# Earlier first norm, reordered loads and unused products in the waits of the first and last image

## The chip, the core and the metric

The kernel runs on one core of a Trainium2 chip. The metric is the device time of one launch in microseconds (us). The engines of the core work side by side and meet at semaphores: TensorE (PE in the rows, its weight loads PEld), VectorE (DVE), ScalarE (ACT), GpSimd (POOL) and SyncE (SP), which here issues the transfers.

## What is computed

A small vision transformer on 64 images. Of each image: 196 patches of 768 numbers are normalised and multiplied by a 768x192 matrix, normalised again and given a class token (197 tokens of 192). Then one attention layer with 12 heads of 64, and a second one with 12 heads of 16 whose weights are corrected by a mixture of eight small experts.

```python
p = x.reshape(B, C, 14, 16, 14, 16).transpose(0, 2, 4, 3, 5, 1).reshape(B, 196, 768)
h = layernorm(layernorm(p, g1, b1) @ W + b, g2, b2)
h = concatenate([cls, h], axis=1)
h = h + attention1(layernorm(h))     # softmax((q k^T) / scale), 12 heads of 64, then w_out
h = h + attention2(layernorm(h))     # qkv + top-2 expert correction, 12 heads of 16, then Wproj
```

## The kernel before

**Stages.** Each image runs through a fixed list of steps, named in the text `ORDER` (L51): X (squares of the patches), EMB (embedding product), LA, LB, LC (two norms on DVE; POOL makes each reciprocal root at L519 and L522), T1 (transpose of the normed tokens), QK.0 to QK.2 (queries and keys), S and PS (sums of squares), N (scaling), SM.0 to SM.5 (maxima of the scores), NT, V.0 and V.1, ST (scores again, with exponentials on ACT), PV, OP, and the same for the second attention with names that end in 2. `@4` behind a step is the PSUM bank in which it starts. Steps marked `+` belong to an image half a pass ahead, `-` and `=` to images one and two half passes behind. A pass holds two images, s=0 and s=1, so 64 images take passes 0 to 31, with a "start" pass ahead that does only X, EMB, LA, LB and LC of the very first image, and a "last" pass behind that does what is left of the last two. The last half of the last pass has nothing but the second attention of image s=1, so its steps only wait for one another.

**Order within an engine.** Every engine walks the same list and runs its own part of each step in that order, waiting on semaphores. On PE each step first waits for its setup (L572 to L581: T1 of the first image for `norm_loaded`, QK.0 for `setup_dve` 3, V.0 for `setup_dve` 4, OP for 5), then for its PSUM banks to be read out (L583 to L585), and then, in its branch, for its operands.

**Loads.** SP issues `emb_loads` (embedding weights, its norm's gain and bias), the first image, `norm_loads` (token bias, the matrix `mats_sb` that holds the identity for transposes, the constants `tokc` of the second norm, `rowc`), `qk_loads` (1536 KB of `w_qk` and three small ones), `v_loads`, the second image and the rest (L447 to L455).

**DVE at the start.** It scales `emb_w` (L907), then in the start pass waits for `qk_loaded` and splits `w_qk` into a high and a low float16 part (`split_rows`, L923 and L926). Then come `constants_of_embedding` (L916, L917; it waits for `norm_loaded` and for PE), EMB (L1038 to L1045), LA (L1055, then `variance`, L1009 and L1012), LB (L1063, L1068, `variance`) and LC (L1018), and directly behind LC of the first image `weights_of_scores` (L937 to L964), which raises `setup_dve` to 3. DVE's part of T1 (L1082) stands behind that. `weights_of_attention2` (L973) stands behind T1 of s=1.

Of the kernel before, what the change touches and what calls it, by code (L numbers as in the profile page):

```python
# [26 lines left out]
B, D, NP = 64, 192, 196  # L27
NT = NP + 1
# [7 lines left out]
ITERS = B // 2  # L36
# [44 lines left out]
WIDE = ("QK", "V", "SM", "ST", "PV")  # L81
QUAD = ("SM2", "ST2")
EBUFS = 4


def banks(p):
# [67 lines left out]
def vit_tower(nc, x_t, w_emb, ln1, ln1_bias, tok_const, tok_bias, w_qk, w_v, w_out, w_gl, w_qkv2, w_lora_b,  # L154
# [4 lines left out]
    with ctx:  # L159
# [10 lines left out]
        emb_w = sb("emb_w", [128, KC, D + 1])  # L170
        ln1_sb = sb("ln1_sb", [128, KC])
        tokc = sb("tokc", [TR, 2, 2, D])
# [5 lines left out]
        qk_w = sb("qk_w", [128, 3, 2 * INNER], F16)  # L178
# [9 lines left out]
        rowc = sb("rowc", [TR, 2 * D + NE + NE * RANK])  # L188
        mats_sb = sb("mats_sb", [128, 261])
# [86 lines left out]
        emb_raw = flat(qk_sq, 128, 0, KC, D)  # L276
        ln1b_raw = flat(qk_sq, 128, KC * D, KC, TR)
# [64 lines left out]
        def wait(eng, now, sig, p, earlier=None, by=1):  # L342


            n = now.count(steps[sig[0]], p, earlier)
            if n is not None:
                eng.wait_ge(sig[1], n * by)
# [19 lines left out]
            body(Pass("last", ITERS))  # L367


        emb_loads = [(emb_raw, w_emb), (ln1_sb, ln1), (ln1b_raw, ln1_bias)]  # L370
        norm_loads = [(tok_b, tok_bias), (mats_sb, mats), (tokc, tok_const), (rowc, row_const)]
        qk_loads = [(scale_sb, scale), (sel_raw[0:64], head_rows[64:128]), (sel_raw[64:128], head_rows[64:128])]
        v_loads, loads = [], [(lorab_raw, w_lora_b), (proj_w[:, 2:3, :], w_proj[:, 2:3, :])]
        for j in range(4):
# [48 lines left out]
        @block.sync  # L423
        def _(sp):
            def load_group(group, loaded):
                for dst, src in group:
                    sp.dma_start(dst[tuple(slice(None) for _ in src.shape)], src).then_inc(loaded, 16)

            def load(n, s):
                sp.dma_start(xb[s][:], x_t[bass.ds(n * 2 + s, 1)].rearrange("b p c t -> (b p) c t")  # L430
                             ).then_inc(x_loaded[s], 16)

            def body(now):
                for kind, s, i in now.steps():
                    if kind == "QK" and i == 0 and now.which in ("first", "middle"):

                        wait(sp, now, pe_sig["EMB"], ("EMB", s, 0))
                        wait(sp, now, xsq_ready, ("X", s, 0))
                        load(now.it + 1, s)
                    elif kind == "OP2":  # L440
                        wait(sp, now, res_ready, ("OP2", s, 0))
                        dst = out[bass.ds(now.image((kind, s, i)) * 2 + s, 1)].rearrange("b t d -> (b t) d")
                        sp.dma_start(dst[1:1 + TO], res[s][0:TO, 0, :]).then_inc(stored[s], 16)
                        sp.dma_start(dst[1 + TO:NT], res[s][0:TO, 1, :]).then_inc(stored[s], 16)
                        sp.dma_start(dst[0:1], res[s][TO:TR, 1, :]).then_inc(stored[s], 16)

            load_group(emb_loads, emb_loaded)  # L447
            load(0, 0)
            load_group(norm_loads, norm_loaded)
            load_group(qk_loads, qk_loaded)  # L450
            load_group(v_loads, v_loaded)
            load(0, 1)
            load_group(loads, consts_loaded)
            sp.wait_ge(bias_cleared, 2)
            load_group(bias_loads, consts_loaded)  # L455
            passes(sp, body)
            for s in range(2):
                sp.wait_ge(stored[s], 48 * (ITERS + s))
# [69 lines left out]
        def _(pe):  # L528
# [38 lines left out]
            def body(now):  # L567
                for p in now.steps():
# [14 lines left out]
                    freed = [(b, *now.previous(users[b], p)) for b in banks(p)]  # L583
                    for sig, q, earlier in dict.fromkeys((*reader(q, b), earlier) for b, q, earlier in freed):
                        wait(pe, now, sig, q, earlier)  # L585
                    if kind == "EMB":
                        pe.wait_ge(x_loaded[s], (now.image(p) + 1) * 16)
                        for t in range(2):
# [308 lines left out]
        def _(dve):  # L897
# [13 lines left out]

            def constants_of_embedding():
                spare = next(b for b in range(8) if b not in [BANK[(k, s, 0)] for k in ("EMB", "T1") for s in range(2)])
                dve.wait_ge(norm_loaded, 16 * len(norm_loads))
                dve.wait_ge(setup_pe, 1)
                nc.vector.tensor_copy(emb_cs[:], psum[0:TR, spare, 0:D])  # L916
                nc.vector.tensor_tensor(emb_b[:], tok_b[:, 0, :], psum[0:TR, spare, D:2 * D], ALU.add  # L917
                                        ).then_inc(setup_dve, 1)
                dve.wait_ge(setup_dve, 2)
# [11 lines left out]
            def split_rows(w, raw):  # L931

                return split_weights(lambda v: w[:, v], raw[:, 0])
# [88 lines left out]
            def body(now):  # L1022
                dve.sem_clear(dve_chain)
                count[0] = 0
                if now.which == "start":
                    dve.wait_ge(qk_loaded, 16 * len(qk_loads))
                    split_rows(qk_w, qk_raw)
                for p in now.steps():
                    kind, s, i = p
                    done = rd_sig[kind][1] if kind in rd_sig else None  # L1030
                    b = BANK[p]
                    if kind == "EMB":
                        if s == 0 and now.image(p) == 0:
                            constants_of_embedding()
# [269 lines left out]
```

## Time and profile before

| what | value |
|---|---|
| median of 3 runs | 3115.53 us (3112.74 to 3116.41) |
| the profiled execution itself | 3115.51 us |
| its span from first to last instruction | 3113.7 us |
| around the span | 1.8 us |
| PE busy | 2965.3 us, 95% |
| DVE busy | 2328.8 us, 75% |
| ACT busy | 1963.5 us, 63% |
| POOL busy | 591.9 us, 19% |
| mean granted clock of TensorE | 0.987 of full speed |

All times in the rows are us from the start of the span. A granted clock of 1.00 is 2.4 GHz, and 0.50 is 1.2 GHz; a value between is a stretch in which it changed. A float32 product shows as two matmul records, a float16 product as one.

### The profile page before, as it was taken

Reading aid. Unit: us, or ns where it says so; the run is one execution under the profiler, and the core shown is the slowest. Engines: PE = TensorE matmul, PEld = TensorE weight load, DVE = VectorE, ACT = ScalarE, POOL = GpSimd, SP = SyncE. Lnnn points to the kernel's source line nnn. Section 1 sums busy time; section 2 is a strip of 40 time slices with the busy share of each in tenths; the row PEclk is TensorE's granted clock in tenths of the full one; section 3 lists DMA queues with packets and bytes.
Section 4 is the critical chain, followed back from the end, with each engine's and each line's share of the span. In section 5 each row is a group of like instructions: output and inputs, shape, how many; then the busy total and the mean of one; then the engine's idle time right before and its main releaser. Section 6 shows DMA issues by size and latency. Waiting matters only on the chain.

```text
span 3113.7 us, 98361 instructions
## 1 busy us (share of the span) xinstructions
PE 2965.3 (95%) x41624; PEld 2430.5 (78%) x41624; DVE 2328.8 (75%) x5441; ACT 1963.5 (63%) x3777; POOL 591.9 (19%) x859
## 2 busy tenths in 40 slices
PE   4899999999999999999999999999999999999996
PEld 4778877877877877877877888778778778778775
DVE  5777777777777777787777777777777777777773
ACT  2566666666666666666666666666666666666663
POOL 2111121121121121121121121121111111111210
PEclk7999999999999999999999999999999999999998
DMA  4000000000000000000000000000000000000000
GB/s 116 9 22 12 22 22 12 21 22 12 21 22 12 22 22 12 22 21 12 22 21 12 22 22 12 22 17 16 22 14 19 22 12 21 22 12 22 14 4 7
DMA packets 28389, 61.28 MB, mean 20 GB/s; under 512 B 4210, under 2 KB 18389, under 8 KB 27958
## 3 DMA queue, kind: packets, MB, share of 16 engines
q1 hardware_dynamic: 27958, 54.98, 6.1%
q8 instruction: 337, 5.52, 0.8%
q14 instruction: 94, 0.77, 0.1%
HBM read 45.29 MB, written 9.68 MB: 18 GB/s over the span
## 4 chain that ended last, share of the span: by engine, by line
PE 59%; DVE 35%; ACT 3%; issue 3%; DMA 0%; SPq 0%; POOL 0%; DVEq 0%; ACTq 0%
PE psum L686 9%; DVE mx L1118 8%; PE psum L695 8%; PE psum L590 8%; PE psum L612 7%; PE psum L622 4%; PE psum L722 4%; PE psum L674 3%; PE psum L656 3%; DVE st L1009 3%; DVE mx L1131 2%; PE psum L725 2%; DVE qk L1210 2%; PE psum L732 2%; DVE late L1227 2%
## 5 line engine op out<-in xcount | busy, mean ns | idle before, releaser
L850 ACT ACTIVATE ebufs<-psum 99x788 f32<-99x788 f32 x768 | 592.0, 823 | 58.1 <-PE psum L674 45.1
L519 POOL TENSOR_TENSOR veps<-mv,eps_ln 99x2 f32<-99x2 f32 x256 | 116.1, 453 | 2274.1 <-DVE mv L1040 1352.3
L1131 DVE TENSOR_REDUCE mx<-psum 99x4 f32<-99x788 f32 x384 | 357.5, 974 | 137.7 <-PE psum L639 137.4
L1118 DVE TENSOR_REDUCE mx<-psum 99x4 f32<-99x788 f32 x384 | 362.9, 974 | 52.1 <-PE psum L631 52.1
L612 PE MATMUL psum<-hn_s,qk_w 128*128 128x197 f16 x3840 | 354.9, 249 | 14.2 <-DVE hn_s L1082 7.2
L612 PEld LDWEIGHTS psum<-hn_s,qk_w 128*128 128x128 f16 x3840 | 323.0, 98 | 34.9 <-DVE qk L1210 19.0
L686 PE MATMUL psum<-ebufs,vx 98*32 98x197 f32 (+1 forms) x6144 | 293.6, 330 | 0.0
L695 PE MATMUL psum<-out_w,qk 128*99 128x192 f32 x1536 | 263.8, 329 | 0.1
L590 PE MATMUL psum<-emb_w,xb 128*99 128x193 f32 x1536 | 263.9, 327 | 0.0
L590 PEld LDWEIGHTS psum<-emb_w,xb 128*99 128x99 f32 x1536 | 249.1, 166 | 1.8 <-issue 1.4
L686 PEld LDWEIGHTS psum<-ebufs,vx 98*32 98x32 f32 (+1 forms) x6144 | 201.2, 110 | 57.5
L695 PEld LDWEIGHTS psum<-out_w,qk 128*99 128x99 f32 x1536 | 245.1, 166 | 0.3 <-issue 0.3
L622 PE MATMUL psum<-v_w,hn_s 128*99 128x384 f16 x1280 | 234.1, 330 | 0.0
L656 PE MATMUL psum<-qh,kh 64*99 64x197 f16 x1536 | 208.5, 255 | 17.5 <-DVE mx L1131 17.0
L1101 DVE TENSOR_TENSOR qk<-qk,ss 128x1182 f32<-128x1182 f32 x64 | 89.0, 1391 | 168.0 <-ACT ss L826 168.0
L802 ACT ACTIVATE qk_sq<-psum 128x788 f32<-128x788 f32 x192 | 158.8, 827 | 70.6 <-PE psum L612 70.6
L656 PE MATMUL psum<-ql,kh 64*99 64x197 f16 x1536 | 202.1, 246 | 0.0
L660 PE MATMUL psum<-neg_t,head_sel 64*99 64x197 f16 x1536 | 201.9, 246 | 0.0
L656 PE MATMUL psum<-qh,kl 64*99 64x197 f16 x1536 | 201.8, 245 | 0.0
L622 PEld LDWEIGHTS psum<-v_w,hn_s 128*99 128x99 f16 x1280 | 155.0, 127 | 47.1
L831 ACT CAST kh<-qk 128x1182 f16<-128x1182 f32 x64 | 75.6, 1181 | 176.4 <-DVE qk L1106 176.4
L1148 DVE TENSOR_TENSOR qk<-psum,rinv 128x394 f32<-128x394 f32 x192 | 108.9, 567 | 102.8 <-ACT rinv L861 62.1
(172 smaller groups left out, 6444.3 us busy)
## 6 DMA issues: line engine op xcount, KB each, us to landing
xb<-x_t SPq DMA_DIRECT2D x64, 591.0 KB, 3.9
out<-h SPq DMA_DIRECT2D x128, 73.5 KB
out<-h SPq DMA_DIRECT2D x64, 0.8 KB
vx<-w_qk SPq DMA_DIRECT2D x2, 384.0 KB, 11.2
qk_sq<-w_emb SPq DMA_DIRECT2D x1, 576.0 KB, 3.7
vx<-w_qk SPq DMA_DIRECT2D x1, 576.0 KB, 8.3
out_w<-w_out SPq DMA_DIRECT2D x8, 72.0 KB
late<-w_lora_b SPq DMA_DIRECT2D x1, 480.0 KB
```

Source lines behind the costliest of these rows:

```text
L590: nc.tensor.matmul(ps(p, slice(0, TR), slice(194 * t, 194 * t + D + 1)), xb[s][:, c, tile_cols(t)], emb_w[:, c, :], start=(c == 0), stop=( ...
L612: mm = nc.tensor.matmul(ps(p, slice(0, 128), slice(at, at + NT), m // 2), qk_w[:, w, f:f + 128], hn_s[s][:, v, c, 0:NT], start=(n == 0), s ...
L622: mm = nc.tensor.matmul(ps(p, slice(0, TR), slice(0, INNER // 2), b), hn_s[s][:, v, c, tile_cols(i)], v_w[:, w, INNER // 2 * b:INNER // 2 ...
L656: nc.tensor.matmul(ps(p, slice(0, TR), slice(NT * t, NT * t + NT), e), left[r], right[r], start=(n == 0), stop=False)
L660: mm = nc.tensor.matmul(ps(p, slice(0, TR), slice(NT * t, NT * t + NT), e), head_sel[r, 2 * i + e, :], neg_t[s][r, 0:NT], start=False, sto ...
L686: mm = nc.tensor.matmul(ps(p, slice(32 * j, 32 * j + 32), slice(NT * (c % 2), NT * (c % 2) + NT), c // 2), left, eb[0:n, j % 2, t, :], sta ...
L695: mm = nc.tensor.matmul(ps(p, slice(0, TR), slice(D * t, D * t + D)), o_t[s][:, m, tile_cols(t)], out_w[:, m, :], start=(m == 0), stop=(m ...
L722: nc.tensor.matmul(o, qkv2_w[:, w, f], hn2_s[s][:, v, c, 0:NT], start=(n == 0), stop=False)
L802: nc.scalar.activation(qk_sq[:, 4 * i:4 * i + 4, :].rearrange("p (b m) t -> p b (m t)", b=2), src, ACT.Square, scale=1 / WS)
L850: nc.scalar.activation(ebuf[n].rearrange("p e a t -> p e (a t)"), psum[0:TR, b + 2 * half:b + 2 * half + 2, 0:2 * NT], ACT.Exp).then_inc(r ...
L1118: nc.vector.tensor_reduce(mx[s][:, :, 2 * i:2 * i + 2].rearrange("p a e -> p e a"), psum[0:TR, b:b + 2, 0:2 * NT].rearrange("p e (a t) -> ...
L1131: nc.vector.tensor_reduce(mx2[s][:, :, at:at + 2].rearrange("p a e -> p e a"), psum[0:TR, b + 2 * half:b + 2 * half + 2, 0:2 * NT].rearran ...
```

## The change

Four things. The token bias is loaded with `emb_loads`, ahead of the first image, and `qk_loads` are issued ahead of what is left of `norm_loads`. DVE's `split_rows` of `w_qk` with its wait moves from the head of the start pass to behind LA, ahead of LB of the first image, and the wait for `norm_loaded` moves there from `constants_of_embedding`. PE runs products without use: in the first images 24 ahead of T1 (s=0), 9 and 2 ahead of QK.0 (s=0, s=1), 9 and 4 ahead of PS, 2 ahead of each of SM.0, 2, 3, 4 and 5 of both, 3 and 1 ahead of NT; in image s=1 of the last pass 3 ahead of each SM2, 8 ahead of NT2, 2 ahead of each ST2 and each PV2, and 4 ahead of OP2. Each is a float32 product of 128x128 weights with 193 columns of `emb_w`, written to the step's own first bank, which the step then overwrites. They stand behind the waits for setup and banks and ahead of the waits for operands.

```diff
+FILL_FIRST = ({"T1": 24, "QK": 9, "PS": 9, "SM": 2, "NT": 3}, {"QK": 2, "PS": 4, "SM": 2, "NT": 1})
+FILL_LAST = {"SM2": 3, "NT2": 8, "ST2": 2, "PV2": 2, "OP2": 4}
...
-        emb_loads = [(emb_raw, w_emb), (ln1_sb, ln1), (ln1b_raw, ln1_bias)]
-        norm_loads = [(tok_b, tok_bias), (mats_sb, mats), (tokc, tok_const), (rowc, row_const)]
+        emb_loads = [(emb_raw, w_emb), (ln1_sb, ln1), (ln1b_raw, ln1_bias), (tok_b, tok_bias)]
+        norm_loads = [(tokc, tok_const), (mats_sb, mats), (rowc, row_const)]
...
             load(0, 0)
+            load_group(qk_loads, qk_loaded)
             load_group(norm_loads, norm_loaded)
-            load_group(qk_loads, qk_loaded)
             load_group(v_loads, v_loaded)
...
+                    fill = 0
+                    if now.image(p) == 0 and i != 1:
+                        fill = FILL_FIRST[s].get(kind, 0) if kind == "SM" or i == 0 else 0
+                    elif now.image(p) == ITERS - 1 and s == 1:
+                        fill = FILL_LAST.get(kind, 0)
+                    for _ in range(fill):
+                        nc.tensor.matmul(ps(p, slice(0, 128), slice(0, D + 1)), emb_w[:, 0, 0:128], emb_w[:, 0, :],
+                                         start=True, stop=True)
...
             def constants_of_embedding():
-                dve.wait_ge(norm_loaded, 16 * len(norm_loads))
                 dve.wait_ge(setup_pe, 1)
...
-                if now.which == "start":
-                    dve.wait_ge(qk_loaded, 16 * len(qk_loads))
-                    split_rows(qk_w, qk_raw)
                 for p in now.steps():
...
+                    if kind == "LB" and s == 0 and now.image(p) == 0:
+
+                        dve.wait_ge(qk_loaded, 16 * len(qk_loads))
+                        split_rows(qk_w, qk_raw)
+                        dve.wait_ge(norm_loaded, 16 * len(norm_loads))
```

## Rows read from the trace of the kernel before

**Rows 1.** Windows: busy us of PE, PEld, DVE, ACT, POOL, granted clock, DMA share, GB/s.

```profile
300.00:800.00 500.00, 487.72 (x6960) 399.47 (x6951) 383.01 (x901) 326.91 (x633) 96.47 (x138) 1.00 0.06 19
```

**Rows 2.** DVE in order of time, 15 to 45 us: start, us, work, idle before.

```profile
19.87 0.96 DVE L923 TENSOR_SCALAR qk_w<-vx 128x1536 f16<-128x1536 f32 x1 [12.92 <-DMA vx<-w_qk]
20.87 1.76 DVE L926 SCALAR_TENSOR_TENSOR qk_w<-vx,qk_w 128x1536 f16<-128x1536 f32 x1
22.54 0.35 DVE L916 COPY emb_cs<-psum 99x192 f32<-99x192 f32 x1
...
26.33 0.25 DVE L1012 BATCH_NORM_AGGREGATE mv<-st 99x2 f32<-99x6 f32 x2
27.66 0.75 DVE L1063 SCALAR_TENSOR_TENSOR h<-lnt,mv,tokc 99x192 f32<-99x192 f32 x2 [1.08 <-POOL rstd L522]
...
32.78 3.82 DVE L940 SCALAR_TENSOR_TENSOR qk_w<-vx,qk_w 64x1536 f16<-64x1536 f32 x1
...
38.15 0.56 DVE L1082 TENSOR_TENSOR hn_s<-psum,hn_s 128x394 f16<-128x394 f32 x1
```

**Rows 3.** PE in order of time, 9 to 96 us, the first image's steps.

```profile
9.56 4.11 PE L590 MATMUL psum<-emb_w,xb 128*99 128x193 f32 x24
...
15.46 0.43 PE L600 MATMUL psum<-emb_w,xss 128*99 128x1 f32 x4
32.02 0.89 PE L563 MATMUL psum<-mats_sb,hn 98*128 98x98 f32 x4 [16.13 <-DVE hn L1018]
38.86 7.61 PE L612 MATMUL psum<-hn_s,qk_w 128*128 128x197 f16 x60 [5.95 <-DVE hn_s L1082]
50.85 1.65 PE L617 MATMUL psum<-ss,mats_sb 128*128 128x394 f32 x2 [4.39 <-DVE ss L1095]
...
95.14 1.65 PE L617 MATMUL psum<-ss,mats_sb 128*128 128x394 f32 x2 [2.26 <-DVE ss L1095]
```

**Rows 4.** DMA issues of 0 to 12 us: KB each.

```profile
tokc<-tok_const SPq DMA_DIRECT2D x1, 297.0 KB
...
rowc<-row_const SPq DMA_DIRECT2D x1, 201.1 KB
...
mats_sb<-mats SPq DMA_DIRECT2D x1, 130.5 KB
...
qk_sq<-tok_bias SPq DMA_DIRECT2D x1, 74.2 KB
```

**Rows 5.** Window of 10 us during the loads, columns as in Rows 1.

```profile
10.00:20.00 10.00, 5.89 (x39) 5.80 (x37) 0.13 (x1) 0.42 (x1) 2.52 (x3) 0.99 1.03 201
```

**Rows 6.** Prices: a weight load (min/median/max ns), and groups of 200 to 2200 us, 80 to 87 us.

```profile
L617 PEld LDWEIGHTS psum<-ss,mats_sb x118: 186/188/191, 235.7 to 2962.6; 128*128 128x128 f32 x118
...
L617 PE MATMUL psum<-ss,mats_sb 128*128 128x394 f32 x84 | 39.0, 546 | 0.0
...
L612 PE MATMUL psum<-hn_s,qk_w 128*128 128x197 f16 x60 | 5.5, 248 | 1.7 <-DVE hn_s L1082 1.3 <-ACT qk L806 0.5
```

**Rows 7.** Windows of 2 us around changes of the granted clock, columns as in Rows 1.

```profile
42.00:44.00 2.00, 2.00 (x16) 1.85 (x15) 0.00 (x0) 1.65 (x5) 0.00 (x0) 0.57 0.00 0
...
64.00:66.00 2.00, 0.79 (x8) 0.26 (x6) 2.00 (x3) 0.00 (x0) 0.00 (x0) 0.55 0.00 0
...
3084.00:3086.00 2.00, 0.15 (x8) 0.00 (x0) 2.00 (x5) 0.00 (x0) 0.00 (x0) 0.75 0.00 0
```

**Rows 8.** DVE in order of time, 67 to 80 us: last maxima of s=0, norm of s=1.

```profile
67.12 1.87 DVE L1118 TENSOR_REDUCE mx<-psum 99x4 f32<-99x788 f32 x2 [0.67 <-PE psum L631]
...
75.82 0.67 DVE L1018 TENSOR_SCALAR hn<-h,mv,rstd 99x192 f32<-99x192 f32 x2 [1.08 <-POOL rstd L522]
...
79.54 0.57 DVE L1082 TENSOR_TENSOR hn_s<-psum,hn_s 128x394 f16<-128x394 f32 x1 [0.36 <-ACT hn_s L796]
```

**Rows 9.** DVE and PE in order of time in the last 30 us.

```profile
3087.18 3.64 DVE L1131 TENSOR_REDUCE mx<-psum 99x4 f32<-99x788 f32 x4 [0.72 <-PE psum L639]
...
3091.18 0.56 PE L552 MATMUL psum<-mats_sb,neg 98*128 98x98 f32 x2 [3.71 <-DVE neg L1139]
...
3106.30 4.13 PE L751 MATMUL psum<-proj_w,late 128*99 128x192 f32 x12 [1.78 <-DVE late L1227]
```

## The prediction

> **What bounds the kernel now.** I read the windows first, then the two ends in order of time. Between 300 and 800 us PE is busy 487.7 of 500 us at full clock [rows 1]; four more such windows up to 2800 us read the same within 1 us. The change touches nothing there, so what it can move is where that saturated stretch starts, and how long the tail behind it is. At the start the end is set by a relay. DVE waits 12.92 us for `w_qk` and splits it before it looks at EMB, which PE finished at 15.9 us (15.46 + 0.43) [rows 2, 3]. Then DVE's norms, `weights_of_scores`, T1 and the queries follow one another. PE waits in that relay again and again, and its clock drops: the 60 products of QK take 7.6 us in the first image and 5.5 busy plus 0.5 waiting in the next, at full clock [rows 3, 6]. The tail is a relay too, of the last image alone [rows 9]. Two readings of the clock matter: it came back only inside the window 42 to 44 us, some 4.9 us after QK's start at 38.86 [rows 3, 7], and it fell inside 64 to 66 and 3084 to 3086 us, where PE was nearly idle for only about two microseconds [rows 7].
>
> **Loads and the moved split.** `tokc`, `rowc` and `mats_sb` are 629 KB, and go behind `w_qk` [rows 4]. At the 201 GB/s of 10 to 20 us [rows 5] that is 3.2 us: `w_qk` lands at about 16.7 instead of 19.87, and the three land near 19.9, since the bytes up to there are the same. `v_loads` and everything SP issues behind them keep their place. The token bias (74.2 KB, 0.4 us) now stands ahead of `emb_loaded` and the first image [rows 4, 5], so PE's setup and EMB end 0.4 us later, EMB at 16.3; DVE can start L916 at about 16.0. From L916 to the end of LA it needs 4.05 us (22.54 to 26.33 + 0.25) [rows 2], so LA ends at 20.1. Both loads are there. The split takes 2.67 us (19.87 to 22.54) [rows 2], and hides the 1.08 us that DVE waited for POOL. LB starts at 22.8 instead of 27.66 [rows 2]: **4.9 us earlier**. If the three norm loads came later than I think, the first 2.7 us of it would be free.
>
> One cost stands against it. L940, on 64 partitions, took 3.82 us where L926, the same operation on 128, took 1.76 [rows 2]; POOL worked beside the first and not beside the second. The moved split now runs exactly while POOL makes the root of LA, which LB needs. If POOL stood still for both instructions, LB would start some 1.1 us later, which is the root's time behind the split; if not, nothing. I take 0.5, for a root that starts between the two instructions. The Trainium skill, SBUF — State Buffer, § Who interferes with whom, says that a VectorE instruction in a two-port mode, or with two SBUF inputs, locks GpSimd's reads out for its whole length. By it the full 1.1 us would be paid. L940 agrees that the two hinder each other, and no row before shows a root beside a split.
>
> `weights_of_scores` follows LC as before, so `setup_dve` 3 comes at about 33.8 instead of 38.15 [rows 2]: **4.4 us** (bounds 3.8 and 4.9).
>
> **Price of a product without use.** None exists before. At full clock EMB's 24 records are 12 such products in 4.11 us, 0.34 each [rows 3]; the other bound is the load of 128 columns of float32 weights, 0.188 us twice, 0.38 [rows 6]. At half clock the 12 records of L751 are six products in 4.13, 0.69 each [rows 9]. I take 0.34 and 0.69, since the columns that stream are EMB's.
>
> **T1, 24 products.** They start when the norm loads land, at 20. PE has been idle for 4 us by then, so I let five run at half clock: 5 x 0.69 + 19 x 0.34 = 9.9 us, to 29.9. LC is ready at about 27, so T1's transposes are 3 us late, but DVE turns to T1 only at 33.8, behind `weights_of_scores`; they need 0.89 us at half clock [rows 3] and a copy on ACT. This cover is 2.5 us. Cost nothing; without the cover it would be 3.
>
> **QK.0, 9 products.** PE waits for `setup_dve` 3 before them, and before the change QK started only 0.7 us after that point. So they lie on the path: 3.1 us at full clock, 4.8 if five are at half clock, less 0.7. PE has idled from T1's transposes (30.5) to 33.8, longer than in the stretches where the clock fell [rows 7], so I take 4.8: QK starts at 38.6, 0.3 earlier than before. It then takes 5.9 to 6.0 instead of 7.61, **gain 1.9 at QK's end**.
>
> **PS, 9 products.** 3.1 us inside the idle 4.39 [rows 3], hidden if warm, 1.8 us over at half clock. The product itself: 39.0 us over 42 pairs, 0.93, instead of 1.65 [rows 3, 6]: gain 0.7.
>
> **SM and NT, s=0.** SM.3 and SM.4 share a bank, so SM.4's two products stand between DVE's reading of SM.3 and the product that DVE waits for. That wait was 0.67 with the four products at half clock [rows 8]; it becomes about 1.15 at full clock, 2.0 at half. SM.0, 2, 3, 5 and NT's three find a maximum of DVE (0.94 us each, 1.87 for two [rows 8]) as cover. Cost 0.5. In exchange NT, V.1 and ST run at full clock, where PE now runs at half from 64 us [rows 7]. What that gives is bounded by DVE: the norm of s=1 is ready at 76.49 (75.82 + 0.67), and the transposed copy reached DVE at 79.54 [rows 8]; transposes and copy need 1.2, so at most 1.9. I take all of it.
>
> **s=1.** PS: 4 products, 1.4 us in an idle 2.26 [rows 3], and again 0.7 for the product. The SM products cost 0.5. Sum **+0.2**, and +0.3 for the embedding beside it.
>
> Start: 1.9 + 0.7 - 0.5 + 1.9 + 0.5 = **4.5 us**.
>
> **The tail.** SM2.1 has SM2.0's banks, so its three products (1.0 us) stand bare in DVE's 0.72 us wait [rows 9]: +0.7 at full clock, +2 at half. NT2's eight (2.7) start when SM2.1 is read, 1.84 us before DVE is done: +0.6. ST2.0 needs NT2's bank and waits for it first, so two products (0.7) lie bare, and its own 32 at full clock give that back. ST2.1, ST2.2 and the three PV2 are much the same, two in the open each, some paid by the faster clock. OP2's four hide in 1.78 us, and OP2 takes 2.1 instead of 4.13 [rows 9]: -2.0. Followed through step by step this gives 0.5 us gained if the clock never falls after 3084 us and 0.9 lost if it falls once between SM2.0 and SM2.1. Taken: **0**.
>
> Sum against the profiled execution: 3115.51 - 4.5 = **3111.0 us**. It lies on the median.
>
> **Rivals.**
> (B) The clock holds from T1 on. If PE's pause before QK.0 doesn't cost the clock, the nine products take 3.1 us, not 4.8: +1.7; without POOL's hindrance +0.5; tail +0.5. Start and tail 7.2: **3108.3**. For it: 24 products just before. Against it: a pause of 3.3 us, and two falls after shorter ones [rows 7].
> (C) The products cost what they bring. The clock comes back only 4.9 us after QK's first product, as it did before [rows 3, 7]: seven at half clock, QK 0.7 us later than in the forecast; it falls again among the SM products (SM.4 and NT cost 2.2, and the 1.9 isn't won), and in the tail (0.9): 4.5 - 0.7 - 1.7 - 1.9 - 0.9, near **3116**, with a fall in one of the two only near 3113.
> (D) The clock is not granted for them, and this is the slower one. Then 24 x 0.69 = 16.6 us run from 20 to 36.6; T1 and its copy reach DVE at 38.0, so all that the norm gained is gone. QK.0's nine cost 6.2, +4.9; PS +1.8; SM.4 and NT of both images +4; the tail +9. Together **3135**. It decides from the point where 24 products take over 13 us, since T1's cover ends there. Against it: EMB's equal products ran at 0.34 [rows 3].
> (E) The change doesn't do what it says, the norm loads landing only after 23 us. It costs a microsecond each, and is part of C.
>
> **How the numbers follow.** Forecast 0.56, B 0.22, C with E 0.17, D 0.05. A measurement of this kernel can tell about 0.2%, 6.2 us: faster means under 3109.3. B is there, and a tenth of the forecast's cases; C within; D above, with a little of C's edge. Faster 0.27, same 0.66, slower 0.07. The range leaves out half of D and the edges: 3107 to 3116.
>
> **What would show it.** L1063 first starts near 23; L926 stays at 1.8; the last T1 filler ends before 33; L612's first record stands over 3 us behind `setup_dve` 3, and its 60 take under 6.2; L617 takes under 1; DVE's waits among the maxima grow to 1.1 or more; L751 of the last image takes 2.1 and the windows near 3084 and 3106 us stay at 1.00. The prediction is wrong if the time is under 3107 (products on the path cheaper than rows say, or the second image gaining more), or over 3116 (clock falls in spite of them).

## The result and the profile after

| what | before | after |
|---|---|---|
| median of 11 runs each | 3115.96 us (3112.74 to 3117.69) | 3122.87 us (3118.31 to 3125.14) |
| ratio of the medians | | 1.0022 (95%: 1.0014 to 1.0030) |
| the profiled execution | 3115.51 us | 3118.31 us, span 3116.5 |
| PE busy | 2965.3 us | 2995.5 us |
| DVE busy | 2328.8 us | 2329.3 us |
| mean granted clock | 0.987 | 0.995 |

The change costs 6.9 us. The clock is granted more fully than before, PE is busy for 30 us more, and the kernel is slower. The profiled execution of after is its fastest run, and nine of the eleven lie above 3122. When the same kernel ran again (`e11_change_again` below), its profiled run took 3123.26 us, which is typical. I therefore read both traces. In the kernel after, all lines of DVE and PE have moved: L923 is L934, L926 is L937, L1063 is L1076, L1082 is L1095, L1118 is L1131, L1125 is L1138, L612 is L624, L617 is L629, L631 is L643, L639 is L651, L751 is L763. The products without use are L596.

DVE of the kernel after in order of time (start, us, line, work, idle before and what ended it) answers to [rows 2]:

```profile
20.32 0.93 DVE L934 TENSOR_SCALAR qk_w<-vx 128x1536 f16<-128x1536 f32 x1
21.28 1.76 DVE L937 SCALAR_TENSOR_TENSOR qk_w<-vx,qk_w 128x1536 f16<-128x1536 f32 x1
23.69 0.75 DVE L1076 SCALAR_TENSOR_TENSOR h<-lnt,mv,tokc 99x192 f32<-99x192 f32 x2 [0.66 <-POOL rstd L526]
...
34.21 0.56 DVE L1095 TENSOR_TENSOR hn_s<-psum,hn_s 128x394 f16<-128x394 f32 x1
```

The move did its work: LB starts at 23.69 instead of 27.66, and DVE reaches T1 3.9 us earlier. PE of the kernel after, same stretch, answers to [rows 3]:

```profile
20.23 9.68 PE L596 MATMUL psum<-emb_w 128*128 128x193 f32 x48 [3.65 <-DMA rowc<-row_const]
...
34.34 6.16 PE L596 MATMUL psum<-emb_w 128*128 128x193 f32 x18 [4.09 <-DVE head_sel L975]
40.30 3.69 PE L624 MATMUL psum<-hn_s,qk_w 128*128 128x197 f16 x40
...
50.62 0.93 PE L629 MATMUL psum<-ss,mats_sb 128*128 128x394 f32 x2 [1.21 <-DVE ss L1108]
...
60.48 1.18 PE L596 MATMUL psum<-emb_w 128*128 128x193 f32 x4 [3.06 <-DVE lnt L1058]
61.59 0.90 PE L643 MATMUL psum<-kh,qh 64*99 64x197 f16 x8
63.23 1.66 PE L596 MATMUL psum<-emb_w 128*128 128x193 f32 x4 [0.75 <-DVE mx L1131]
64.82 0.57 PE L643 MATMUL psum<-kh,qh 64*99 64x197 f16 x4
65.31 1.65 PE L596 MATMUL psum<-emb_w 128*128 128x193 f32 x4
```

T1's 24 are hidden. QK.0's nine take all that the move gave: the queries start at 40.30, 1.4 us later than before, and only their faster clock brings them back, so that PS stands where it stood. Then come the maxima. DVE in the same kernel, against [rows 8]:

```profile
62.20 1.86 DVE L1131 TENSOR_REDUCE mx<-psum 99x4 f32<-99x788 f32 x2 [0.24 <-PE psum L643]
65.43 0.98 DVE L1131 TENSOR_REDUCE mx<-psum 99x4 f32<-99x788 f32 x1 [1.37 <-PE psum L643]
67.51 0.98 DVE L1131 TENSOR_REDUCE mx<-psum 99x4 f32<-99x788 f32 x1 [1.10 <-PE psum L643]
70.74 0.98 DVE L1131 TENSOR_REDUCE mx<-psum 99x4 f32<-99x788 f32 x1 [2.25 <-PE psum L643]
72.82 0.98 DVE L1131 TENSOR_REDUCE mx<-psum 99x4 f32<-99x788 f32 x1 [1.10 <-PE psum L643]
73.84 0.19 DVE L1138 TENSOR_SCALAR neg<-mx 99x48 f32<-99x48 f32 x1
```

Before, DVE waited once among its six maxima, for 0.67 us, and the stretch from the first maximum to the negation took 6.2 us. Now it waits four times, 5.8 us in all, and the stretch takes 11.6. The windows show why each wait is so long (us, PE busy, PEld, DVE, ACT, POOL, granted clock, DMA share, GB/s):

```profile
60.00:62.00 2.00, 1.52 (x10) 1.09 (x12) 1.82 (x3) 1.24 (x2) 0.75 (x2) 0.75 0.00 0
...
64.00:66.00 2.00, 2.00 (x9) 1.30 (x9) 0.63 (x2) 0.00 (x0) 0.00 (x0) 0.50 0.00 0
...
72.00:74.00 2.00, 2.00 (x9) 1.54 (x9) 1.14 (x2) 0.00 (x0) 0.00 (x0) 0.50 0.00 0
74.00:76.00 2.00, 2.00 (x13) 1.75 (x12) 1.62 (x7) 0.33 (x1) 0.00 (x0) 0.84 0.01 4
...
60.00:75.00 15.00, 12.70 (x53) 9.07 (x54) 8.45 (x12) 1.24 (x2) 0.75 (x2) 0.54 0.00 0
```

PE idled from 57.4 to 60.48, since SM.0's two products may not start before DVE has read the bank (L1058), and the clock fell to 1.2 GHz. It stayed there up to the window 74 to 76, through the five pairs and NT's three, which were there to keep it up. PE was not idle much in that time (the last row). The tail of the kernel after answers to [rows 9]:

```profile
3087.79 1.46 PE L596 MATMUL psum<-emb_w 128*128 128x193 f32 x6 [2.54 <-DVE mx L1144]
...
3089.68 2.30 PE L596 MATMUL psum<-emb_w 128*128 128x193 f32 x6
...
3092.26 2.88 PE L596 MATMUL psum<-emb_w 128*128 128x193 f32 x16
3094.97 0.34 PE L556 MATMUL psum<-mats_sb,neg 98*128 98x98 f32 x2
...
3111.10 2.19 PE L763 MATMUL psum<-proj_w,late 128*99 128x192 f32 x12 [0.20 <-DVE late L1240]
```

OP2 takes 2.19 us instead of 4.13, and the products ahead of it cost more than that.

**Where the time goes**, by the start of one instruction of each stage (us, profiled executions). `e4_no_sm` is the change without the pairs ahead of the SM steps, `e8_ahead_both` a version with other places for the products; both come below.

| stage | before | move alone (e1) | e4 | after | change again (e11) | e8 |
|---|---|---|---|---|---|---|
| first query product | 38.86 | 35.22 | 38.88 | 40.30 | 39.40 | 36.34 |
| PS | 50.85 | 46.92 | 49.09 | 50.62 | 49.60 | 46.63 |
| negation of the maxima | 69.02 | 65.09 | 66.53 | 73.84 | 73.30 | 64.74 |
| the same, second image | 115.97 | 110.50 | 112.64 | 120.45 | 121.47 | 110.73 |
| first QK2 product | 125.52 | 120.04 | 122.47 | 129.61 | 130.62 | 119.88 |
| last image's QK2 | 3079.74 | 3074.33 | 3076.98 | 3080.92 | 3084.57 | 3073.15 |
| OP2 of the last image | 3106.30 | 3100.85 | 3108.41 | 3111.10 | 3116.01 | 3097.09 |
| last work of DVE | 3110.54 | 3105.08 | 3110.71 | 3113.40 | 3118.31 | 3099.39 |

From before to e11, which is the fair pair, the start loses 5.1 us (125.52 to 130.62), the long middle nothing, and the tail 2.9 (30.8 to 33.7 us from QK2 to the end): 7.8 for a difference of the medians of 6.9. The profiled run of after is 4.95 us shorter than e11, in three places. The second image's maxima ran at full clock there and at half in e11 (1.0). Between the first and the last of these QK2 products after is 2.6 shorter: 1.35 of it lies where the clock fell at 3028 us in e11, as it did at 3020 in before, and did not in after, and 1.1 near 3052, where it fell in both and came back later in e11. The tail is 1.3 shorter, where the clock fell once more in e11, in ST2.

### The profile page after: what moved, and what is told of

Read it like the earlier page. It is cut to its first block, busy times and chain, and to the rows that moved or that the text cites. A ratio compares the mean times of both kernels' runs of the same rounds, so it can differ in the third digit from the quotient of the medians.

```text
span 3116.5 us, 98765 instructions
## 1 busy us (share of the span) xinstructions
PE 2995.5 (96%) x41834; PEld 2458.1 (79%) x41834; DVE 2329.3 (75%) x5441; ACT 1963.5 (63%) x3777; POOL 594.1 (19%) x859
## 4 chain that ended last, share of the span: by engine, by line
PE 60%; DVE 34%; ACT 3%; issue 3%; POOL 0%; DMA 0%; SPq 0%; DVEq 0%; ACTq 0%
PE psum L698 9%; PE psum L707 8%; DVE mx L1131 8%; PE psum L602 8%; PE psum L624 7%; PE psum L686 4%; PE psum L634 4%; PE psum L734 4%; PE psum L668 3%; DVE st L1020 3%; PE psum L737 2%; DVE qk L1223 2%; DVE mx L1144 2%; PE psum L744 2%; PE psum L629 2%
## 5 line engine op out<-in xcount | busy, mean ns | idle before, releaser
L1131 DVE TENSOR_REDUCE mx<-psum 99x4 f32<-99x788 f32 x384 | 363.2, 974 | 56.2 <-PE psum L643 56.2
L624 PE MATMUL psum<-hn_s,qk_w 128*128 128x197 f16 x3840 | 352.9, 248 | 9.1 <-DVE hn_s L1095 1.6
L624 PEld LDWEIGHTS psum<-hn_s,qk_w 128*128 128x128 f16 x3840 | 321.3, 97 | 29.6 <-DVE qk L1223 19.0
```

Source lines behind the costliest of these rows:

```text
L624: mm = nc.tensor.matmul(ps(p, slice(0, 128), slice(at, at + NT), m // 2), qk_w[:, w, f:f + 128], hn_s[s][:, v, c, 0:NT], start=(n == 0), s ...
L1131: nc.vector.tensor_reduce(mx[s][:, :, 2 * i:2 * i + 2].rearrange("p a e -> p e a"), psum[0:TR, b:b + 2, 0:2 * NT].rearrange("p e (a t) -> ...
```

## The experiments

Each kernel is compared with runs of the kernel before on the same chip; e1 to e4, e5 to e8 and e9 to e12 ran together. Between these groups the ratios are to be compared, not the medians. e8 rests on 4 runs, e10 and e12 on 5 each, the others on 10 or 11. The diffs are against the kernel after.

| run | what is in it | median, us | before, us | ratio (95%) |
|---|---|---|---|---|
| e1_move_alone | loads and split, no products | 3111.19 | 3117.25 | 0.9981 (0.9972 to 0.9990) |
| e2_move_first | move, all products of the first images | 3120.26 | 3117.25 | 1.0006 (0.9998 to 1.0015) |
| e3_move_last | move, products of the last image | 3112.99 | 3117.25 | 0.9986 (0.9977 to 0.9995) |
| e4_no_sm | the change without SM's pairs | 3114.19 | 3117.25 | 0.9990 (0.9981 to 0.9999) |
| e5_sm_alone | move, SM's pairs | 3114.41 | 3115.99 | 1.0000 (0.9990 to 1.0009) |
| e6_t1_ps | move, T1's 24, PS's 9 and 4 | 3110.31 | 3115.99 | 0.9984 (0.9974 to 0.9993) |
| e7_ahead_first | move, products ahead of the waits | 3109.50 | 3115.99 | 0.9980 (0.9971 to 0.9989) |
| e8_ahead_both | e7, and in the last image 13 products ahead of the waits and 9 behind | 3103.72 | 3115.99 | 0.9962 (0.9947 to 0.9977) |
| e9_t1_qk_ps | e6 and QK.0's 9 and 2 | 3112.76 | 3116.95 | 0.9987 (0.9978 to 0.9996) |
| e10_hold_more | e8, a few products moved and added | 3102.24 | 3116.95 | 0.9955 (0.9942 to 0.9967) |
| e11_change_again | the change | 3122.83 | 3116.95 | 1.0016 (1.0007 to 1.0025) |
| e12_ahead_again | e8 | 3103.56 | 3116.95 | 0.9954 (0.9940 to 0.9967) |

### Which part costs: e1 to e4

The theory after the result was that the products lie on the path, SM's above all. The rivals were the move, the first images' products as a whole, and the tail.

```diff
# e1_move_alone
-FILL_FIRST = ({"T1": 24, "QK": 9, "PS": 9, "SM": 2, "NT": 3}, {"QK": 2, "PS": 4, "SM": 2, "NT": 1})
-FILL_LAST = {"SM2": 3, "NT2": 8, "ST2": 2, "PV2": 2, "OP2": 4}
+FILL_FIRST = ({}, {})
+FILL_LAST = {}
```

> The change without any product without use: only the moved split and the reordered loads. My theory: the move is worth some 4 us by itself (LB of the first image started 3.97 us earlier in the changed kernel) and the products lose more than that, so this kernel is faster than before by 3 to 5 us, near 3112. Rival A (the move brings nothing, since something behind it, a load or an engine, is late anyway): within 1 us of before, 3116. Rival B (the steady stretch suffers from the new offset between engines): slower than before by 2 us or more.

The move alone is 6.1 us faster than before. So the part of the change without any product is a gain, a larger one than I had given the whole, and the products turn it round. It is also a little more than the 3 to 5 us expected of it.

```diff
# e2_move_first
-FILL_LAST = {"SM2": 3, "NT2": 8, "ST2": 2, "PV2": 2, "OP2": 4}
+FILL_LAST = {}
```

> The change without the products in the last image. My theory: the greater part of the loss is made in the first image, where the changed kernel came to its steady stretch 4.1 us late although LB was 3.97 us early; so this one stays 3 to 5 us slower than before, near 3120, and the last image is worth 2 to 4 us. Rival (the tail makes the loss): this one is at before or under it, 3112 to 3116.

9.1 us slower than e1. The first images' products cost that much.

```diff
# e3_move_last
-FILL_FIRST = ({"T1": 24, "QK": 9, "PS": 9, "SM": 2, "NT": 3}, {"QK": 2, "PS": 4, "SM": 2, "NT": 1})
+FILL_FIRST = ({}, {})
```

> The change without the products in the first image. My theory: gain of the move, 4 us, less what the tail's products cost, 2 to 4 us: 3113 to 3116. Rival (the tail makes the loss): 3120 or more. If the tail's products cost nothing in themselves: equal to the move alone, near 3112.

1.8 us slower than e1: the tail's products cost a little, in the profiled run 3.0 (33.7 us from QK2 to the end, against 30.75 in e1).

```diff
# e4_no_sm
-FILL_FIRST = ({"T1": 24, "QK": 9, "PS": 9, "SM": 2, "NT": 3}, {"QK": 2, "PS": 4, "SM": 2, "NT": 1})
+FILL_FIRST = ({"T1": 24, "QK": 9, "PS": 9, "NT": 3}, {"QK": 2, "PS": 4, "NT": 1})
```

> The change with only the products ahead of SM.0, 2, 3, 4 and 5 taken out, in both images. My theory: between the end of DVE's N.3 and NT of the first image the changed kernel lost 5.4 us, all to pairs of products at half clock in front of the maxima, so this one is 4 to 6 us faster than the changed kernel, near 3117.5. Rival (the clock would fall there anyway and the same time is lost on NT and V.1, as it was before): only 3 us or less of it come back, 3120. Rival (QK.0's nine products are the loss): no more than 1 us comes back.

Its ratio is 0.9990, and the change's are 1.0022 and 1.0016: the difference is 8 to 10 us, where I had expected 4 to 6. Twenty products, two ahead of each of ten SM steps, make the difference between a gain and a loss. At 0.34 each they are 6.8 us of work, so they are paid in full and more. The other products together cost e4 3.0 us against e1 of the same group.

The clock fell in e4 among the maxima too. DVE of e4, and one of its windows:

```profile
64.63 1.86 DVE L1131 TENSOR_REDUCE mx<-psum 99x4 f32<-99x788 f32 x2 [0.67 <-PE psum L643]
```

```profile
60.00:62.00 2.00, 0.61 (x6) 0.24 (x4) 2.00 (x3) 0.00 (x0) 0.00 (x0) 0.50 0.00 0
```

Its stretch from the first maximum to the negation (60.34 to 66.53) takes 6.2 us even so, as before. So the fall of the clock by itself costs nothing there; it costs when the pairs run at it.

### Is it the clock or the place: e5, e6, e9

```diff
# e5_sm_alone
-FILL_FIRST = ({"T1": 24, "QK": 9, "PS": 9, "SM": 2, "NT": 3}, {"QK": 2, "PS": 4, "SM": 2, "NT": 1})
-FILL_LAST = {"SM2": 3, "NT2": 8, "ST2": 2, "PV2": 2, "OP2": 4}
+FILL_FIRST = ({"SM": 2}, {"SM": 2})
+FILL_LAST = {}
```

> The move, and of all products only the pairs ahead of SM.0, 2, 3, 4 and 5 of both images. My theory: these pairs alone are the loss, standing after DVE's reading of the bank and before the product that DVE waits for, at half clock; the stretch from the first maximum to its negation takes some 11.6 us instead of 6.2, and the total is 6 to 10 us over the move alone (3111), 3117 to 3121. Rival (they hurt only together with the others, since those let the clock fall at another moment): within 3 us of the move alone.

The median is 3114.41, under the 3117 to 3121 that I had expected, and 4.1 us above e6 of the same group. Beside the other products the same pairs cost 8 to 10 us. Seven runs lie from 3111.9 to 3115.4, three from 3117.6 to 3119.0. The profiled one is the fastest, and there the clock held: PE had idled for 2.12 us ahead of SM.0's pair, against 3.06 in the kernel after. Whether this is why it held is not shown. Its DVE and one of its windows:

```profile
61.10 0.98 DVE L1131 TENSOR_REDUCE mx<-psum 99x4 f32<-99x788 f32 x1 [0.44 <-PE psum L643]
...
64.55 0.98 DVE L1131 TENSOR_REDUCE mx<-psum 99x4 f32<-99x788 f32 x1 [1.32 <-PE psum L643]
```

```profile
62.00:64.00 2.00, 0.92 (x8) 0.63 (x5) 1.06 (x2) 0.00 (x0) 0.00 (x0) 1.00 0.00 0
```

And its PE, around SM.4 and SM.5:

```profile
63.28 0.92 PE L596 MATMUL psum<-emb_w 128*128 128x193 f32 x4 [1.08 <-DVE mx L1131]
64.14 0.37 PE L643 MATMUL psum<-kh,qh 64*99 64x197 f16 x4
64.44 0.92 PE L596 MATMUL psum<-emb_w 128*128 128x193 f32 x4
```

At full clock a pair and its four products take 1.16 us (63.28 to 64.44), and a maximum takes 0.98. So every step is slower than the maximum that should cover it, and SM.4 has no cover at all. The stretch takes 7.9 us instead of 6.2: 1.7 us are paid in the first image even when the clock stays up, and 1.3 in the second (from PS to the negation, 21.0 us against 19.7 in e1). At half clock a step takes 2.08 (63.23 to 65.31 in the kernel after) and the stretch 11.6. The place costs 1.7 us, and the half clock makes the pairs 3.7 dearer on top.

```diff
# e6_t1_ps
-FILL_FIRST = ({"T1": 24, "QK": 9, "PS": 9, "SM": 2, "NT": 3}, {"QK": 2, "PS": 4, "SM": 2, "NT": 1})
-FILL_LAST = {"SM2": 3, "NT2": 8, "ST2": 2, "PV2": 2, "OP2": 4}
+FILL_FIRST = ({"T1": 24, "PS": 9}, {"PS": 4})
+FILL_LAST = {}
```

> The move, and of all products only the 24 ahead of T1 and the 9 and 4 ahead of PS, which lie inside idle stretches of TensorE. My theory: QK.0 starts as early as in the move alone (35.2 us in its trace) and PS runs at full clock: 1 to 2 us under the move alone, 3109 to 3110. Rival (products in a wait cost even there, through DVE or ACT): at the move alone or over it, 3111 to 3113.

0.9984, where e1 has 0.9981 without a product. In the trace PS starts 0.5 us and the negation 1.2 us earlier than in e1. T1's and PS's products are hidden, and what they bring is below what the medians can tell.

```diff
# e9_t1_qk_ps
-FILL_FIRST = ({"T1": 24, "QK": 9, "PS": 9, "SM": 2, "NT": 3}, {"QK": 2, "PS": 4, "SM": 2, "NT": 1})
-FILL_LAST = {"SM2": 3, "NT2": 8, "ST2": 2, "PV2": 2, "OP2": 4}
+FILL_FIRST = ({"T1": 24, "QK": 9, "PS": 9}, {"QK": 2, "PS": 4})
+FILL_LAST = {}
```

> The move with the products ahead of T1 and PS, as in an earlier run (3110.3), and now the 9 and 2 ahead of QK.0 too. My theory: they start only when setup_dve 3 arrives and so lie on the path, 3.1 to 6.2 us less the 0.7 that was waited anyway, and give 1.9 back at most: 1.5 to 2.5 us over that run, 3112 to 3112.8. Rival (they pay by keeping the clock for what follows): at that run or below, 3110 or less.

0.9987 against e6's 0.9984: by the times alone the two can't be told apart. By the traces they can. PE of e9, and of e6 in the second fence:

```profile
34.33 4.85 PE L596 MATMUL psum<-emb_w 128*128 128x193 f32 x18 [4.47 <-DVE head_sel L975]
39.02 3.58 PE L624 MATMUL psum<-hn_s,qk_w 128*128 128x197 f16 x40
```

```profile
34.91 4.88 PE L624 MATMUL psum<-hn_s,qk_w 128*128 128x197 f16 x40 [4.42 <-DVE hn_s L1095]
```

The nine take 4.69 us to the first query product. They save 1.3 us in its 40 records (4.88 against 3.58), PS starts 2.8 us later than in e6 (49.22 and 46.41), and the first QK2 product 3.4 (122.29 and 118.86). They stand behind the wait for `setup_dve` 3, and so they fill none of the 4.4 us of idle time that the fence shows; they begin where it ends.

### Products ahead of the waits: e7, e8, e10, e12

If the place is the cause, the same kind of products must pay when they run inside the idle time. In e7 they stand ahead of the step's waits, write to a bank that nobody uses then, and wait only for that bank's last reader.

```diff
# e7_ahead_first
-FILL_FIRST = ({"T1": 24, "QK": 9, "PS": 9, "SM": 2, "NT": 3}, {"QK": 2, "PS": 4, "SM": 2, "NT": 1})
-FILL_LAST = {"SM2": 3, "NT2": 8, "ST2": 2, "PV2": 2, "OP2": 4}
+FILL_FIRST = ({}, {"PS": 4})
+FILL_LAST = {}
+WAIT_FIRST = {('T1', 0, 0): (30, 7), ('QK', 0, 0): (17, 7), ('PS', 0, 0): (11, 7), ('SM', 0, 0): (7, 7), ('SM', 0, 2): (2, 7), ('SM', 0, 4): (3, 7), ('NT', 0, 0): (3, 7), ('SM', 1, 2): (3, 7), ('SM', 1, 4): (4, 7)}
...
                 for p in now.steps():
...
+                        if q is not None:
+                            wait(pe, now, *reader(q, spare_bank), earlier)
+                        for _ in range(count):
+                            nc.tensor.matmul(psum[0:128, spare_bank, 0:D + 1], emb_w[:, 0, 0:128], emb_w[:, 0, :],
+                                             start=True, stop=True)
                     if s == 0 and now.image(p) == 0:
```

> The move, and in the first image products of the same kind in other places: ahead of the waits for setup and banks instead of behind them, in bank 7, which nobody uses by then (30 ahead of T1, 17 of QK.0, 11 of PS, 7 of SM.0, 2 of SM.2, 3 of SM.4 and NT; for s=1 3 and 4 ahead of SM.2 and SM.4, and the 4 of PS as they were). My theory: the place makes the loss and not the idea; the clock never falls, QK takes 6 us, PS 0.9, NT and V.1 1.8: 3 to 5 us under the move alone, 3106 to 3108. Rival (TensorE's lowered clock costs nothing, since DVE and ACT set the end of each step anyway): within 1 us of the move alone, 3111. Rival (products delay what follows them wherever they stand): 3113 or more.

6.5 us faster than before, but so is the move alone: 0.9980 here, 0.9981 in e1. I had expected 3 to 5 us more than the move gives, and the rival that a lowered clock costs nothing in the first image fits the median. In the profiled run its loads landed late (the split starts at 21.87, in e1 at 20.64), and the first QK2 product starts at 120.04 in both, so 1.2 us may be gained behind the split; the medians can't tell it. PE of e7:

```profile
30.08 5.74 PE L590 MATMUL psum<-emb_w 128*128 128x193 f32 x34
...
36.50 3.57 PE L640 MATMUL psum<-hn_s,qk_w 128*128 128x197 f16 x40 [0.68 <-DVE hn_s L1111]
```

Seventeen products, nearly twice the change's nine, cost nothing: they end before the operand comes, and the queries run at full clock. The SM steps and NT show the place best: 22 products ahead of the waits of both images (24 behind them in the change) cost nothing that the medians show, and in the profiled run at most the 0.5 us by which the stretch of the first image's maxima is longer (6.7 us, with its clock at half). From T1 on DVE (35.80) to the negation (64.71) e7 takes 28.9 us, e1 30.6, the kernel after 39.6.

```diff
# e8_ahead_both: e7, and
-FILL_LAST = {}
-WAIT_LAST = {}
+FILL_LAST = {"NT2": 5, "OP2": 4}
+WAIT_LAST = {('SM2', 1, 1): (6, 3), ('ST2', 1, 1): (4, 3), ('PV2', 1, 2): (3, 4)}
```

> As the run before, and in the last image 6 products ahead of the bank wait of SM2.1 and 4 ahead of that of ST2.1 in bank 3, 3 ahead of that of PV2.2 in bank 4, and 5 of NT2 and 4 of OP2 behind their waits as in the change. My theory: OP2 at full clock gives 2.0 us, NT2 and ST2 0.7, nothing lies on the path: 2 to 3 us under the run before, 3104 to 3105. Rival (the tail's products push what they stand ahead of): equal or slower than the run before.

3103.72, a ratio of 0.9962, and 5.8 us below e7, more than the 2 to 3 that I had expected of the tail. A part of it is e7's own tail, which took 32.1 us in its profiled run, 1.3 more than before. PE of e8 in its tail:

```profile
3077.20 0.38 PE L667 MATMUL psum<-qk 32*99 32x197 f16 x8 [1.15 <-ACT qk L915]
3077.51 2.23 PE L590 MATMUL psum<-emb_w 128*128 128x193 f32 x12
3079.98 0.80 PE L667 MATMUL psum<-qk 32*99 32x197 f16 x16 [0.25 <-issue]
...
3097.09 2.19 PE L779 MATMUL psum<-proj_w,late 128*99 128x192 f32 x12 [0.19 <-DVE late L1256]
```

Six products fill the time in which the kernel before had 2.41 us of idle PE, and SM2.1 follows DVE's reading at once. From QK2 to the end the tail takes 26.2 us, against 30.8 before and 33.7 in e11. The place is not the only difference from the change here: e8 has 22 products in its tail, the change 33, and the 5 of NT2 and the 4 of OP2 stand behind their waits in e8 as in the change. OP2 takes 2.19 us in both.

```diff
# e10_hold_more: e8, and
-FILL_FIRST = ({}, {"PS": 4})
-WAIT_FIRST = {('T1', 0, 0): (30, 7), ('QK', 0, 0): (17, 7), ('PS', 0, 0): (11, 7), ('SM', 0, 0): (7, 7), ('SM', 0, 2): (2, 7), ('SM', 0, 4): (3, 7), ('NT', 0, 0): (3, 7), ('SM', 1, 2): (3, 7), ('SM', 1, 4): (4, 7)}
+FILL_FIRST = ({}, {"QK": 6, "PS": 4})
+WAIT_FIRST = {('T1', 0, 0): (30, 7), ('QK', 0, 0): (17, 7), ('PS', 0, 0): (11, 7), ('SM', 0, 0): (7, 7), ('SM', 0, 2): (3, 7), ('SM', 0, 4): (2, 7), ('NT', 0, 0): (4, 7), ('SM', 1, 2): (3, 7), ('SM', 1, 4): (4, 7)}
```

> The kernel with products ahead of the waits in both images (3103.7 in its first timing), with 6 in place of none ahead of QK.0 of s=1 and the counts of SM.2, SM.4 and NT set to the idle times seen (3, 2, 4). In its trace the clock still fell between 74 and 81 us, over QK of s=1, and once inside SM. My theory: 0.5 to 2 us more, 3102 to 3103, since QK of s=1 is hidden behind weights_of_attention2 on DVE and only SM's and NT's part is on the path. Rival (the clock over QK of s=1 sets the end): 3100 to 3101. Rival (the products ahead of QK.0 of s=1 delay it): 3104 or more.

In e7 and e8 the clock still fell among the maxima. Windows of e8, and behind them of e10:

```profile
60.00:62.00 2.00, 2.00 (x10) 1.71 (x6) 1.49 (x2) 0.00 (x0) 0.00 (x0) 0.55 0.00 0
62.00:64.00 2.00, 2.00 (x13) 1.52 (x13) 1.16 (x2) 0.00 (x0) 0.00 (x0) 0.60 0.00 0
```

```profile
58.00:60.00 2.00, 1.30 (x10) 0.87 (x12) 1.87 (x3) 0.00 (x0) 0.00 (x0) 1.00 0.00 0
60.00:62.00 2.00, 1.98 (x16) 1.54 (x16) 1.66 (x2) 0.00 (x0) 0.00 (x0) 1.00 0.00 0
```

In e10 it held, DVE waited 0.47 us in the stretch, and it took 6.0 us, less than before. But in e12, which is e8's kernel again, it held there too, with the same 0.47 and 6.0, so this is the run and not the new counts. What e10 alone shows is a clock that holds over QK of the second image, from 74 us on; it falls there in e7, e8 and e12. The median is 3102.24, the lowest of all, but only 1.3 us below e12 of the same group, and the runs of the two overlap (3101.3 to 3104.5 and 3101.1 to 3104.6). In the profiled runs the split also starts at 20.09 in e10 and at 22.11 in e12, by the loads. Whether e10's extra products are worth anything is not settled.

### The two again: e11, e12

> The changed kernel itself once more, on the chip of these runs. My theory: 3121 to 3125, with a profile in which the maxima of s=0 and in most executions those of s=1 too run at half clock. Rival (the second image's maxima stay at full clock in all executions and the spread comes from the tail): the stretch from PS to the negation of s=1 takes 21.0 us as in the first profile.

> The kernel with products ahead of the waits in both images once more, for its interval, which rests on 4 timed runs so far. Both theories: 3102.5 to 3104.5, 12 to 13 us under before.

The change repeats its result, 3122.83, and e8's kernel its own, 3103.56. In e11 the second image's maxima ran at half clock too. DVE and one window:

```profile
118.50 0.98 DVE L1131 TENSOR_REDUCE mx<-psum 99x4 f32<-99x788 f32 x1 [2.06 <-PE psum L643]
120.45 0.98 DVE L1131 TENSOR_REDUCE mx<-psum 99x4 f32<-99x788 f32 x1 [0.97 <-PE psum L643]
```

```profile
117.00:119.00 2.00, 2.00 (x9) 1.31 (x9) 0.50 (x1) 0.00 (x0) 0.00 (x0) 0.50 0.03 8
```

In the profiled run of after the first of these waits was 1.32 us, at full clock. This is one of the places from which the spread of the change's runs comes.

## Why the prediction was wrong

The forecast was 3111, the result 3122.87, seven microseconds above the range's upper end and on the side that had a chance of 0.07. Step by step:

**The loads and the move: right.** The split starts at 20.32, LA ends at 20.4 (20.15 + 0.25; 20.1 was expected), `rowc` lands at 20.2 (19.9). The token bias was to cost 0.4 us ahead of EMB. PE's first product starts at 6.75 here and at 5.61 before, 1.1 later; over the profiled runs of all kernels with this order of loads it starts at 5.92 to 7.03, so 0.3 to 1.4 later than in the one trace of before. POOL's root stood beside the split, as thought:

```profile
20.48 0.81 POOL L523 TENSOR_TENSOR veps<-mv,eps_ln 99x2 f32<-99x2 f32 x1 [1.87 <-DVE mv L1023]
21.37 2.22 POOL L526 TENSOR_TENSOR rstd<-veps,half_neg 99x2 f32<-99x2 f32 x1
26.24 0.19 POOL L523 TENSOR_TENSOR veps<-mv,eps_ln 99x2 f32<-99x2 f32 x1 [2.65 <-DVE mv L1023]
26.51 0.69 POOL L526 TENSOR_TENSOR rstd<-veps,half_neg 99x2 f32<-99x2 f32 x1
```

The same two operations take 3.03 us beside the split and 0.88 without it, and LB waited 0.66 us for the second. POOL's first operation ends 0.04 us behind DVE's first, its second 0.55 us behind DVE's second (23.59 and 23.04), nearly its own length of 0.69. So the root ran for the most part when the split was over. The rule of the Trainium skill, SBUF — State Buffer, § Who interferes with whom, that such a VectorE instruction, once it holds the ports that the two share, shuts GpSimd's reads out for its whole length, agrees with these rows. The wait of 0.66 us lies between my 0.5 and the bound of 1.1: the first of the two operations was done when the split's first instruction ended, and only the root was left behind it. The gain at LB is 4.0 us, 4.4 was predicted, and at T1 on DVE 3.9 instead of 4.4.

**What the move alone is worth: not in the sum.** The sum took the move and the products of QK.0 together, and the text never says what the move would give by itself. In e1 it gives 3.9 us at PS, 5.5 at QK2 and 6.1 in the median. A part whose edits can be made apart needs its own total, and then the next part is judged by whether it adds to that. By this measure the nine products of QK.0 were a loss in the prediction's own numbers (4.4 us at T1, 1.9 left behind them), and e9 against e6 shows it, with 2.8 us at PS.

**T1, QK.0, PS: near in size.** T1's 24 took 9.7 us (9.9 predicted) and were hidden. QK.0's nine took 4.7 us in e9 and 5.96 in the profiled run of after, where all of them ran at half clock (4.8 predicted), so that the gain at PS was 0.2 us there, 1.8 in e4 and 1.3 in e11, for a forecast of 1.9. The queries then took 5.9 us (5.9 to 6.0). PS took 0.93 (0.93). Up to SM.0 the forecast had 2.6 us of gain, and e4, which is the change without SM's pairs, has 2.5 at the negation.

**SM: the step that failed.** The prediction charged 0.5 us for the first image's pairs: SM.4's alone, with "SM.0, 2, 3, 5 and NT's three find a maximum of DVE (0.94 us each, 1.87 for two [rows 8]) as cover". The charge is 6.8 us, by e11 against e4 at the negation (73.30 and 66.53), and 8.2 by the first QK2 product, with the second image's pairs (130.62 and 122.47); 0.5 of both was there already at PS. Three errors stand in it.
- The cover. A pair starts when DVE has read the bank, and DVE's next maximum needs the product behind the pair. So the time to compare was pair plus product plus the switch against one maximum, for each step in turn, and not the pair against a maximum. A pair at the prediction's own price is 0.68, and the four products of SM take 0.30 (64.14 to 64.44 in e5): 0.98 against 0.94, no room at all.
- The price. A pair takes 0.85 us from its start to the next product, 0.42 a product, and not the 0.34 of a group of twelve: this is beyond even the bound by the load of the weights, 0.38 by [rows 6], which I had set aside.
- The clock. SM.0's pair waits for EMB's bank, PE idles for 3.06 us, and the clock falls. At half clock a step takes 2.08 us against a maximum of 0.98, and PE, busy for 1.25 to 2.00 us of each 2, was not given the full clock until all five pairs were done and NT's three nearly. Rival C had this fall, and priced it at 2.2 us and a gain not won, where the stretch grew by 5.4 (11.6 instead of 6.2).

**The 1.9 us from a warm NT, V.1 and ST: wrong too.** In the kernel after they came at full clock (V.1 took 1.79 us instead of 3.41), behind a negation that was 4.8 us late. DVE and ACT there, against the last two lines of [rows 8]:

```profile
80.65 0.67 DVE L1029 TENSOR_SCALAR hn<-h,mv,rstd 99x192 f32<-99x192 f32 x2 [1.08 <-POOL rstd L526]
82.19 1.17 ACT L798 ACTIVATE qk_sq<-xb 128x1182 f32<-128x1182 f32 x1
83.77 0.57 DVE L1095 TENSOR_TENSOR hn_s<-psum,hn_s 128x394 f16<-128x394 f32 x1 [0.88 <-ACT hn_s L808]
```

From the norm's end to T1 on DVE it is 2.45 us (81.32 to 83.77), before 3.05: the gain is 0.6. The forecast let transposes and copy take 1.2, but on ACT the squares of the patches (L798) stand ahead of that copy (L808, from 83.27). In e10, where the clock held throughout, it is 2.46 as well. So 1.3 of the forecast's 4.5 us could not come even without the pairs.

**The tail: wrong by 2 to 3 us** (32.5 us in the profiled run of after and 33.7 in e11, against 30.8). e11 against before: 11.4 to 14.1 us from QK2 to NT2 (+2.7), 15.1 to 17.3 from NT2 to OP2 (+2.2), and OP2 with its end 4.2 to 2.3 (-1.9). OP2 is as predicted. SM2 and NT2 were priced at 1.3 us, since SM2.2's three were taken as covered; they ran at half clock, 2.3 us, behind SM2.1's, so that DVE waited for SM2.2 as well (0.71 us in the profiled run of after). The loss from one fall of the clock was named as 0.9; it was 1.7 with one (after) and 2.9 with two (e11).

**The rivals.** C, that the products cost what they bring, is the one whose mechanism came: the clock falls in both places. It was given 3116, for it used the same price of SM. D, the slower one, needed a clock that is not granted for such products at all; T1's 24 show that it is. So the mechanism that made the kernel slower, a pair between two dependent steps of a relay, was in the text as a detail, and I gave it no case of its own. The range could not hold it.

**What would show it.** L1076 at 23.7, L937 at 1.76, T1's last product before 33, the 60 products at 5.9 and L629 at 0.93 came out as written. DVE's waits grew to 1.1 or more, as written, but four of them instead of one. L763 took 2.19, and the windows of 3084 and 3106 us stayed at 1.00 in the profiled run of after, but that of 3088 fell to 0.66.

## What to carry to other kernels

Work that is to keep TensorE's clock up belongs ahead of the wait that makes the idle time, into a PSUM bank that is free then; behind that wait it lies on the path from its first product on. Products behind an earlier wait were hidden here too (T1, PS, OP2), where the wait that ended last was the one for operands. With products ahead of the waits the kernel became 12 to 15 us faster than before (0.9954 to 0.9962), and with the pairs behind them 6 to 7 us slower, with the same move in both. Of the 12 to 15 about 6 are the move's (e1), nothing that the times can tell is the first image's products' (e7), and the rest is the tail's. So in the first image the place decided what the products cost, and a full clock brought time that the medians can tell in the tail alone, where the counts differ too. Before anything is put into a relay between two engines, add up the whole turn of one engine, with the new work in it, and compare it with the turn of the other; and cost each separable part of a change against the version that has the others and not this one.

## What the runs showed of the hardware

- Short groups of float32 products are dearer than long ones at the same clock: 0.42 us each in a pair (0.85 from a pair's start to the next product in e5), 0.34 in EMB's twelve.
- A half clock can outlast much activity, as rows show it: in the kernel after PE was busy 12.7 us of the 15 from 60 us on, and had a granted clock of 0.54 there.
- Full clock is no measure of speed. After has 0.995 against 0.987, and takes longer. In e4 the maxima ran beside PE at 0.50 for the same 6.2 us as before.
- POOL's two small operations beside a split on DVE took 3.03 us, and 0.88 without one.
- From run to run the clock falls or holds in the same places: at 3020 to 3028 us in before, at 3028 in e11, not in after. That is 1.35 us of spread which no edit touched.
